# A three-layer interaction tower: chunk 1 loaded by ScalarE's queue, the context first, chunk 0 stored in two parts, the last layer 2 in another bank

## What is computed

```python
e = stack([tbl_f[ids[:, f]] for f in range(39)], axis=1)      # (512, 39, 16)
x0 = xk = e
for idx, (W, b) in enumerate([(w0, b0), (w1, b1), (w2, b2)]):  # W: (39, fk, 128)
    z = relu(einsum('bhd,bkd,hks->bsd', x0, xk, W) + b[None, :, None])
    if idx != 2:
        xk = z[:, :64, :];  direct.append(z[:, 64:, :])
    else:
        direct.append(z)
logit = sum(concatenate(direct, axis=1), axis=-1)             # (512, 256)
h = relu(concatenate([logit, dense_ctx], axis=1) @ W_top1 + b_top1)
h = relu(h @ W_top2 + b_top2)
y = h @ W_top3
```

## Time and profile before

| | |
|---|---|
| median of three runs | 658.29 us (657.54 to 659.74) |
| the profiled execution | 657.38 us |
| its span, first to last instruction | 655.5 us |
| mean granted TensorE clock | 0.99 |
| TensorE busy | 608.5 us, 93% |
| VectorE busy | 550.0 us, 84% |
| GpSimd busy | 537.1 us, 82% |
| ScalarE busy | 409.3 us, 62% |
| moved by DMA | 90.29 MB, mean 138 GB/s |
| chain that ended last | PE 40%, POOL 36%, ACT 10%, issue 6%, DVE 5%, DMA 2% |

### The profile page before, as it was taken

How to read it: one execution, slowest core, us unless ns; L and a number is a source line. 1 busy time by engine, 2 the same in 40 slices (tenths; PEclk the granted TensorE clock), 3 DMA queues, 4 the chain that set the end, 5 groups by cost and what they waited for, 6 DMA issues and landing times.

```text
span 655.5 us, 6276 instructions
## 1 busy us (share of the span) xinstructions
PE 608.5 (93%) x1996; PEld 376.1 (57%) x1996; DVE 550.0 (84%) x620; ACT 409.3 (62%) x551; POOL 537.1 (82%) x325
## 2 busy tenths in 40 slices
PE   0178899999999999999999999999999999999998
PEld 0035466656666566656666566666566665655563
DVE  0376899898989898998989898999989898969750
ACT  2043758677676758576766757586776667584622
POOL 6786799898989899998989998999989895746530
PEclk9979899999999999999999999999999999999999
DMA  6687883838363645648374645547383745420000
GB/s 221 150 180 222 173 249 77 250 76 248 70 209 85 167 127 130 197 82 245 71 229 91 188 90 153 160 111 216 76 250 67 213 93 176 102 64 1 0 0 0
DMA packets 64043, 90.29 MB, mean 138 GB/s; under 512 B 46624, under 2 KB 49568, under 8 KB 60042
## 3 DMA queue, kind: packets, MB, share of 16 engines
q1 hardware_dynamic: 57402, 87.89, 49.5%
q0 software_dynamic: 5120, 1.29, 2.0%
q10 hardware_dynamic: 1488, 0.72, 0.4%
HBM read 87.31 MB, written 8.95 MB: 147 GB/s over the span
## 4 chain that ended last, share of the span: by engine, by line
PE 40%; POOL 36%; ACT 10%; issue 6%; DVE 5%; DMA 2%; SPq 0%; ACTq 0%; DVEq 0%
POOL low L378 29%; PE z L701 21%; PE z L718 10%; POOL gat L368 7%; PE z L733 6%; ACT x L464 6%; ACT high L444 2%; DVE prod L607 2%; ACT r L488 1%; DMA spread<-x_rows 1%; DVE x L616 1%; DVE prod L588 1%; DVE base L642 1%; DVE low L650 1%; PE x L778 1%
## 5 line engine op out<-in xcount | busy, mean ns | idle before, releaser
L378 POOL TENSOR_TENSOR low<-prod,high 128x1024 fp32r<-128x1024 f32 (+1 forms) x160 | 380.9, 2398 | 56.4 <-ACT high L444 55.1
L607 DVE TENSOR_TENSOR prod<-spread,x 128x1024 f32<-128x1024 f32 x256 | 308.1, 1214 | 35.3 <-ACT x L464 33.6
L701 PE MATMUL z<-prod,w_sb 128*128 128x512 f32 (+2 forms) x608 | 290.6, 598 | 37.3 <-DVE prod L588 32.8
L444 ACT ACTIVATE high<-prod 128x1024 fp32r<-128x1024 f32 (+1 forms) x160 | 167.8, 1058 | 124.0 <-DVE prod L607 99.8
L718 PE MATMUL z<-high,high_w_L 128*128 128x512 f32 (+1 forms) x448 | 203.7, 455 | 4.0 <-ACT high L444 2.8
L701 PEld LDWEIGHTS z<-prod,w_sb 128*128 128x128 f32 (+2 forms) x608 | 115.4, 190 | 122.8 <-issue 103.4
L368 POOL DMA_INDIRECT gat<-table_dram,index x160 | 155.5, 972 | 36.5 <-issue 33.9
L733 PE MATMUL z<-low,high_w_L 128*128 128x512 f32 (+1 forms) x448 | 182.1, 487 | 3.5 <-POOL low L378 1.9
L718 PE MATMUL z<-high,low_w_L 128*128 128x512 f32 (+1 forms) x448 | 179.0, 400 | 0.0
L464 ACT ACTIVATE x<-z,bias_sb 64x512 f32<-64x512 f32 (+1 forms) x180 | 116.3, 646 | 14.8 <-PE z L701 7.4
L733 PEld LDWEIGHTS z<-low,high_w_L 128*128 128x128 f32 (+1 forms) x448 | 82.8, 190 | 68.9 <-issue 44.7
(11 more groups left out here) (37 smaller groups left out, 73.5 us busy)
## 6 DMA issues: line engine op xcount, KB each, us to landing
spread<-x_rows SPq DMA_DIRECT2D x15, 1792.0 KB, 7.1
spread<-x_rows SPq DMA_DIRECT2D x32, 768.0 KB, 11.0
spread<-x_rows SPq DMA_DIRECT2D x16, 1024.0 KB, 7.3
x_rows<-x_rows SPq DMA_DIRECT2D x16, 390.0 KB
x0base<-x_rows SPq DMA_DIRECT2D x47, 78.0 KB
gat<-table_dram,index POOLq DMA_INDIRECT x160, 3.7
x_rows<-gat SPq DMA_DIRECT2D x31, 72.0 KB, 2.3
wt_sb<-wt_dram SPq DMA_DIRECT2D x2, 512.0 KB, 17.4
```

The source lines that it names most:

```text
L378: pool.tensor_tensor(low[0:rows, h, 0:k, :], prod[0:rows, slot(c, kind, g), 0:k, :], high[0:rows, h, 0:k, :].bitcast(F32), ALU.subtract).t ...
L444: act.activation(high[0:rows, split_slot(c, kind, g), 0:k, :], prod[0:rows, slot(c, kind, g), 0:k, :], ACT.Copy).then_inc(high_ready, 1)
L607: dve.tensor_tensor(prod[0:rows, slot(c, kind, g), :, :], spread[0:rows, c % 2, g, :].unsqueeze(1).to_broadcast([rows, k, N]), x[0:rows, : ...
L701: last = pe.matmul(z[:, :], w[0:rows, at + j, :], prod[0:rows, slot(c, kind, g), j, :], start=g == 0 and j == 0, stop=closes and j == k - 1)
```

## The change

- **Chunk 0 in two stores.** The first five gathers count on a semaphore of their own; SP stores their rows early (`store_soon`) and loads from them the part of the layer 0 factors that they hold, 13 of 39 rows in each of three blocks (`load_soon`). The later stores and first loads leave these out. ScalarE stores the same five gathers for the second copy.
- **Chunk 1 by ScalarE's queue.** Between its split in layer 0 of chunk 0 and its x1 copies, ScalarE waits for the gathers of chunk 1, stores both copies, waits until they have landed and issues the repeat. After the x1 copies and the relu it issues base and `spread0` of chunk 1. SP goes on from the `spread` pieces of chunk 0 to those of chunk 1.
- **Layer 0's weights** are folded behind the gathers of chunk 0 and split last of the three.
- **Context first.** Its weights, bias and input are loaded at the start; TensorE multiplies them before anything else, VectorE adds the bias and keeps the result in `ctx_part`, and at the end adds it to each of the four sums, before a relu on ScalarE.
- **The last layer 2** sums into z0 instead of z2, so it waits for the layer 0 output of chunk 15 and not for ScalarE's relu of chunk 14. The x2 copies before it are shared by ScalarE and VectorE; that relu comes two groups later and its sum on VectorE at group 5 instead of 3.
- The top weights are loaded in step 4; the last product is made and copied in two halves.

```diff
+TOP_AT = 4
+SOON = 5
+SOON_ROWS = SOON * FPT - T0
+def gathers_until(c):
+    return 16 * (GAT * (c // GBUF + 1) - (SOON if c % GBUF == 0 else 0))
+def stored_until(c):
+    return 64 * (c // 2 + 1) + (16 if c % 2 == 0 else 0)
...
+            def store_soon():
+                sp.wait_ge(gathered_soon, 16 * SOON)
+                first = x0_dram[0, 0:1, 0:1]
+                sp.dma_start(bass.AP(first.tensor, first.offset, [[D, P], [FPT * N, SOON], [1, D]]),
+                             gat[:, 0, 0:SOON, :]).then_inc(stored_soon, 16)
+            def load_soon():
+                sp.wait_ge(stored_soon, 16)
+                row = x0_dram[0, 0:1, 0:1]
+                for j in range(DPT):
+                    sp.dma_start(spread0[j * F:j * F + SOON_ROWS, :, :].rearrange("p t n -> p (t n)"),
+                                 bass.AP(row.tensor, row.offset, [[N, SOON_ROWS], [1, T0 * N]])
+                                 ).then_inc(spread0_soon, 16)
...
             sp.dma_start(bias_sb[:, :], biases).then_inc(bias_in, 16)
+            sp.dma_start(wt1c_sb[:, :], wt1[2 * P:, :]).then_inc(ctx_in, 16)
+            sp.dma_start(ctx_sb[:, :], ctxT).then_inc(ctx_in, 16)
+            sp.dma_start(bt1_sb[:, :], bt1).then_inc(ctx_in, 16)
...
+            store_soon()
+            load_soon()
             store_x0(0, (0,))
...
             for p in range(len(PIECES)):
                 load_spread(0, p)
-            store_x0(1)
-            load_base(1)
-            repeat_x0(1)
-            load_spread0(1)
             for p in range(len(PIECES)):
                 load_spread(1, p)
...
+            def repeat_second():
+                act.wait_ge(x0_stored[1], stored_until(1))
+                row = x0_dram[1, 0:1, 0:1]
+                to = x0_dram[1, 2 * F:2 * F + 1, 0:1]
+                act.dma_start(bass.AP(to.tensor, to.offset, [[N, F], [F * N, COPIES - 2], [1, N]]),
+                              bass.AP(row.tensor, row.offset, [[N, F], [0, COPIES - 2], [1, N]])
+                              ).then_inc(x0_copied[1], 16)
+            def load_second():
+                for j in range(DPT):
+                    row = x0_dram[1, (F - j * T0) % F:(F - j * T0) % F + 1, 0:1]
+                    act.dma_start(x0base[j * F:(j + 1) * F, :], bass.AP(row.tensor, row.offset, [[N, F], [1, N]])
+                                  ).then_inc(base_in, 16)
+                act.wait_ge(prod_done, PROD_NUMBER[0, "L0", G0 - 1])
+                act.wait_ge(x0_copied[1], 16)
+                row = x0_dram[1, 0:1, 0:1]
+                act.dma_start(spread0[:, :, :].rearrange("p t n -> p (t n)"),
+                              bass.AP(row.tensor, row.offset, [[N, P], [1, T0 * N]])).then_inc(spread0_in, 16)
...
-            act.wait_ge(w0_folded, 1)
-            split_weights("L0", R0, w0_sb[:, 2 * SPLIT["L0"][0]:2 * SPLIT["L0"][0] + 2, :].rearrange("p t s -> p (t s)"))
...
-            store_first_again()
+            store_x0(0, (1,))
             load_first()
+            act.wait_ge(w0_folded, 1)
+            split_weights("L0", R0, w0_sb[:, 2 * SPLIT["L0"][0]:2 * SPLIT["L0"][0] + 2, :].rearrange("p t s -> p (t s)"))
...
-                if i >= 2:
+                if i == NCH:
+                    shared_copies(i - 1, x2, z1, "L1", 1, x2_ready)
+                    relu1(i - 1, 2)
+                elif i >= 2:
...
+                        if i == NCH and g == 2:
+                            relu2(i - 2)
...
                     if kind == "L0" and i == 0:
-                        first_copies(x1, z0, "L0", 0, x1_ready)
+                        store_x0(1, (0, 1))
+                        repeat_second()
+                        shared_copies(0, x1, z0, "L0", 0, x1_ready)
                         relu0(i, 2)
+                        load_second()
...
+            dve.wait_ge(ctx_in, 16 * 3)
+            for m in range(H1 // P):
+                dve.wait_ge(ctx_done, m + 1)
+                dve.tensor_scalar(ctx_part[:, m, :], ctx_sum[m], bt1_sb[:, m:m + 1], 0.0, ALU.add, ALU.add)
+            dve.wait_ge(gathered[0], gathers_until(0))
             dve.wait_ge(w0_in, 32)
...
-            pe.wait_ge(r0_ready, NCH)
-            pe.wait_ge(r1_ready, NCH)
-            for m in range(H1 // P):
-                pe.matmul(h1_sum[m][:, :], wt1c_sb[:, m * P:(m + 1) * P], ctx_sb[:, :], start=True, stop=False)
             for c, kind, gs in stages_of(NCH):
                 sum_stage(c, kind, gs)
```

More of the change, by code:

```diff
@@ L465, in copies, with shared_copies @@
                                    bias=bias_sb[k:k + end - at, layer:layer + 1]).then_inc(ready, 1)
-            def first_copies(to, z, kind, layer, ready):
-                act.wait_ge(mm_done, stage_end(0, kind))
+            def shared_copies(c, to, z, kind, layer, ready):
+                act.wait_ge(mm_done, stage_end(c, kind))
+                if c >= 1:
+                    ringed, tiled = products_of(c - 1, "L1" if kind == "L0" else "L2", range(G1))
+                    act.wait_ge(prod_done, ringed)
+                    if tiled:
+                        act.wait_ge(tile_prod, tiled)
                 for tile in range(2):
@@ L595, in wait_factors @@
                 if g == 0:
-                    dve.wait_ge(ready, (2 + FPT) * (c + 1) + 2)
+                    dve.wait_ge(ready, (2 + FPT) * (c + 1) + (4 if kind == "L2" and c == NCH - 1 else 2))
                 for p, (at, _) in enumerate(PIECES):
@@ L609, in product, with shared_copies @@
                                   x[0:rows, :, :], ALU.mult).then_inc(prod_done, 1)
-            def first_copies(to, z, kind, layer, ready):
-                dve.wait_ge(mm_done, stage_end(0, kind))
+            def shared_copies(c, to, z, kind, layer, ready):
+                dve.wait_ge(mm_done, stage_end(c, kind))
+                if c >= 1:
+                    ringed, tiled = products_of(c - 1, "L1" if kind == "L0" else "L2", range(G1))
+                    dve.wait_ge(prod_done, ringed)
+                    if tiled:
+                        dve.wait_ge(tile_prod, tiled)
                 for tile in range(2):
@@ L750, in sum_stage @@
                     sum_low(c, kind, gs[-1], DONE[c, kind, gs[-1]] == closing)
+            pe.wait_ge(ctx_in, 16 * 3)
+            for m in range(H1 // P):
+                pe.matmul(ctx_sum[m], wt1c_sb[:, m * P:(m + 1) * P], ctx_sb[:, :],
+                          start=True, stop=True).then_inc(ctx_done, 1)
             pe.wait_ge(w1_in, 32)
@@ L782, in _ @@
                 pe.wait_ge(h2_ready, k + 1)
-                last = pe.matmul(z0[0:1, :], wt3_sb[:, k:k + 1], h2[:, k, :],
-                                 start=(k == 0), stop=(k == H2 // P - 1))
-            last.then_inc(y_done, 1)
+                for n in range(2):
+                    last = pe.matmul(y_sum[n], wt3_sb[:, k:k + 1], h2[:, k, n * B // 2:(n + 1) * B // 2],
+                                     start=(k == 0), stop=(k == H2 // P - 1))
+                    if k == H2 // P - 1:
+                        last.then_inc(y_done, 1)
 def layer_rows(w, gs):
```

148 lines of the change are left out of this document (91 added, 57 removed).

## The result

The changed kernel takes **662.06 us** (median of 17 runs, 660.05 to 663.76) against 658.39 beside it (17 runs): ratio 1.0057, 95% interval 1.0045 to 1.0069. That is 3.7 us slower, where 657.6 (a change of +0.2) was forecast, and 1.1 us above the upper end of the range. The profiled execution took 661.74 us with a span of 659.9, 4.4 more than before.

What follows compares the result with a forecast made beforehand. GpSimd's lows and gathers set the pace of chunks 2 to 14, so only front and tail count: 657.38 + 4.4 lost in front - 4.2 won in the tail = 657.6 us; range 648.8 to 661.

Steps and rivals of the forecast that it cites:

- Landing of chunk 0's stores: Front, chunk 0: both stores landed at 21.5 us instead of 22.11, bounds 21.1 and 22.6.
- From there to SP's large loads: Front: 9.4 us instead of 11.94, 2.5 off for bytes loaded early; large loads issued at 30.9 us.
- The landing of chunk 1's stores follows these loads by 15.9: Front, ScalarE's queue: stores held up behind SP's large loads issued at 30.9, landing at 46.8 us.
- the two main cases: Chunk 1's stores held up until 46.8 us (forecast, chance 0.50), or landed at 37.9 to 41 (chance 0.28).
- Packet for packet: DMA queues: small packets get at best one turn per large packet, leaving at least 2100 waiting when large loads finish.
- The first rival: Chunk 1's small store packets are not held up, landing at 37.9 to 41; 650 us taken; chance 0.28.
- From the landing to product 0 of chunk 1: Front: repeat, x1 copies and layer 1 of chunk 0 follow the landing, 19.6 us to product 0 at 66.4.
- Factors of chunk 1 just in time: Front: chunk 1's layer 0 factors land at 65 us, with 1.4 us of reserve before product 0.
- the second rival: Chunk 1's factors also come too late, at 69 us; 7.1 us lost in front, 660.3 us; chance 0.22.
- Late fold, 0.8 sooner: Front: folding layer 0's weights behind chunk 0's gathers lets those gathers end 0.8 us sooner.
- End, 4.2 won: Tail: last layer 2 ends 3.9 us sooner, last y copy gives 0.3; 4.2 us won, bounds 2.3 and 4.8.
- Clock, bank and shared copies: Tail: full PE clock without 16-row passes, another sum bank avoiding a relu wait, x2 copies in 3.13 instead of 4.01 us.

Runs made afterwards that it cites:

- e14: Changed kernel with chunk 0's early store kept but the three early loads of layer 0 factors removed; 660.15 us, ratio 1.0033.
- e3: Changed kernel, but ScalarE issues only chunk 1's four stores; SP waits for their landing and issues repeat, base and factors; 654.22 us, ratio 0.9934.
- e4: Kernel before the change with only the edits of the end, context first included; 654.33 us, ratio 0.9937.
- e12: No early store or loads, SP loads chunk 1, its stores between second and third large load; layer 0's weights folded and split early; 652.84 us, ratio 0.9910.
- e9: The e4 kernel with sixteen passes of 16 rows put back in front of the last layer 2; 656.62 us, ratio 0.9976.
- e8: The e4 kernel with the last x2 copies made by ScalarE alone; 655.64 us, ratio 0.9961.

## Why the prediction was wrong

Point by point, the forecast beside what came:

- **What bounds the kernel, and the place of the change**: right. Front and end add up, the middle is untouched (36.36 us a chunk).
- **Landing of chunk 0's stores, 21.5 (bounds 21.1 to 22.6): 24.30. This step failed.** The prediction counted the early loads only as something that SP must issue ahead of the stores, and gave them no time as 0.56 MB that is in the DMA queues when the stores arrive. They were issued 1.5 us ahead of the stores, and took 58 us of DMA engines instead of 21 (39 at 0.55). The early store alone lands at 19.96 (e14), better than I had it.
- **From there to SP's large loads, 9.4: 10.4.** The 2.5 us that I took off for the bytes already loaded is 2.0 (10.43 against 12.45 in e14), and without them the way is 12.45 and not 11.94. Together the large loads came at 34.73 instead of 30.9, 3.8 late, which is later than in the kernel before: the early loads save 2.0 behind the landing and make the landing 4.3 later. Nor did the first product start 1.5 us sooner: it came at 30.58, 2.2 later than before, and at 26.87, 1.5 sooner, in e14.
- **The landing of chunk 1's stores follows these loads by 15.9: 15.4.** Right in size, and it is the term on which the two main cases differed; the reason given for it holds only in part. "Packet for packet" would have left at least 2100 small packets waiting at the end of the large loads. In fact 1357 of 2560 had gone by 46.5 us (last section), and the rest still came behind them. That the landing nevertheless came as forecast is in part luck. The first rival (landing at 38 to 41) is refuted in its time, and half right in its mechanism.
- **From the landing to product 0 of chunk 1, 19.6: 19.7**, ScalarE's idle stretch, TensorE's and the 1.75 us included. e3 shows that it is this wait and not the landing that costs.
- **Factors of chunk 1 just in time**: in time, as far as the trace shows; the second rival (too late) isn't seen, since VectorE waits for the base copy. The reserve of 1.4 us can't be read from it. (The rival's 50.6 + 12 is 62.6, not 62.7; nothing hangs on it.)
- **Context matmuls, additions and weights of the top at nothing**: nothing in e4 speaks against it; they were not run one by one. Beside the four additions of the changed kernel, 9.67 to 15.46 us, each gather took 0.93 to 0.95.
- **Late fold, 0.8 sooner**: a fold beside a gather can cost 0.8, but whether it does is chance (e4, e12).
- **End, 4.2 won: 3.6 in the trace, 4.1 by the medians of e4.** Clock, bank and shared copies as told; the last layer 2 won 3.4 instead of 3.9. It began 0.15 later than forecast (625.24, with the shift of 7.94), and VectorE reached the second half of the tiled product 0.27 later (628.21), for which TensorE waits.

In one line: front forecast +4.4 and measured +8.0, of which 3.8 is the large loads' issue, less 0.5 for the shorter way to the landing and some tenths of rest; end forecast -4.2 and measured -3.6. The sum had both signs and the wait at the head of ScalarE right. It failed in the early loads: 2.8 of the 3.8 is the landing, for which they were counted by their issue alone, and 1.0 the way from there, where their bytes were taken off in proportion.

## What to carry to other kernels

A wait for a DMA's landing belongs on an engine that has nothing to compute behind it: a landing near 50 to 52 cost 7.3 us more at the head of ScalarE than on SP. A small transfer's place in the order counts against everything that is issued in front of it, here on its own queue (about 4 us for each load of 768 to 1024 KB) and on the other one alike, so small stores that others wait for go ahead of large loads, as long as the large loads themselves are not needed sooner. And a load that is "only an issue" must be costed by what it occupies: before one is split off, look to how many partitions it writes.

## What the hardware showed

- Packets of 14 KB to three blocks of 13 neighbouring partitions took 1.5 us each, to every ninth partition 0.77, to 117 partitions 0.55.
- A queue of small packets is not served evenly beside large ones. Chunk 1's stores on ScalarE's queue (q10) beside SP's large loads (q1), in 38.5 to 40.5 and in 41 to 46.5 us:

```profile
q1 hardware_dynamic: 84, 0.42, 76.3%
q10 hardware_dynamic: 1024, 0.06, 38.2%
...
q1 hardware_dynamic: 191, 1.29, 98.8%
q10 hardware_dynamic: 176, 0.01, 3.6%
```

In the first stretch 12 small packets went to each large one, in the second 1 to 1. Of the 2560 packets of this queue 1181 had gone by 41 us, about one of the two copies; 1173 went from 46.5 to 49, when the large loads were all but over (37 packets). The prediction assumed 1 to 1 throughout. By the Trainium skill (DMA: Bandwidth & Descriptors, Queues, rings and completion order) a turn is some 9 to 17 descriptors. If a turn of SP's queue moved one large row, the first stretch agrees and the second doesn't; turns are not seen in the trace, which has one descriptor to a packet. What switches between the two is open; that second stretch is why the landing still waited for the large loads.
- The half clock came back when the 16-row passes did (e9: 0.50 in 624 to 626 us, where e4 has 1.00 from 615 to 640). What it costs in a usual run is open: ten runs of that kernel spread over 7.8 us, eight of them over 2.5, and ten of e8, the same end but for the passes and the copies, over 2.7. The profiled one of the two slow ones had lost 3 us before the passes.
